# The key side's band moves from TensorE to GpSimd, and the values come one period later

## The reference, cut to what matters

```
h = shift_token(x); q, k, v = split(h @ wqkv)          # 8 heads of 64
q, k = rotary_xpos(l2norm(q) * qs, l2norm(k) * ksc)
sim  = einsum(q * 8, [keys of the window before, own window])   # windows of 64
sim  = where((i < j) | (i > j + 64) | (j == -1), -max, sim)     # the band
x    = x + (softmax(sim) @ v) @ wo
h    = layernorm(shift_token(x)) @ w1 + b1; a, g = split(h)
x    = x + (a * gelu(g)) @ w2 + b2
```

## Time and profile before

| | |
|---|---|
| median of the runs | 1264.93 us (1263.29 to 1266.61) |
| span of the profiled execution | 1264.4 us, 0.5 us under that median; its own device time is not listed apart |
| TensorE busy | 1158.7 us, 92% of the span |
| VectorE busy | 986.2 us, 78% |
| ScalarE busy | 829.0 us, 66% |
| GpSimd busy | 443.5 us, 35% |
| chain that ended last | TensorE 51% of the span, VectorE 4%, ScalarE 2%, issue 1% |

### The profile page before, as it was taken

How to read it: one execution, slowest core, us unless ns; L and a number is a source line. 1 busy time by engine, 2 the same in 40 slices (tenths; PEclk the granted TensorE clock), 3 DMA queues, 4 the chain that set the end, 5 groups by cost and what they waited for, 6 DMA issues and landing times.

```text
span 1264.4 us, 36707 instructions
## 1 busy us (share of the span) xinstructions
PE 1158.7 (92%) x15602; PEld 682.3 (54%) x15602; DVE 986.2 (78%) x1556; ACT 829.0 (66%) x1229; POOL 443.5 (35%) x582
## 2 busy tenths in 40 slices
PE   4498999899999999688999999999999999999985
PEld 3133434343435555455666666666666666666662
DVE  7868695868768888796877887788778877887755
ACT  3498898889887877535556656665666566656641
POOL 2203221211206447855533333333333333333310
PEclk8599999999999999988999999999999999999997
DMA  3113121020113331100201110111111111101102
GB/s 105 34 24 136 39 101 35 18 101 18 63 56 125 127 136 69 50 18 19 80 21 27 24 30 20 28 27 23 27 27 23 28 23 27 28 23 28 27 6 67
DMA packets 37329, 59.78 MB, mean 47 GB/s; under 512 B 6416, under 2 KB 12464, under 8 KB 37168
## 3 DMA queue, kind: packets, MB, share of 16 engines
q1 hardware_dynamic: 35760, 56.61, 15.1%
q10 hardware_dynamic: 1408, 0.84, 0.3%
HBM read 22.58 MB, written 16.78 MB: 31 GB/s over the span
## 4 chain that ended last, share of the span: by engine, by line
PE 51%; DVE 4%; ACT 2%; issue 1%; DVEq 0%; ACTq 0%
PE psum L1338 9%; PE psum L1474 7%; PE psum L1427 6%; PE psum L1449 5%; PE psum L1413 5%; PE psum L1348 4%; PE psum L1358 3%; PE psum L1500 3%; PE psum L1435 2%; PE psum L1398 2%; PE psum L1370 2%; ACT ffn_probs L1657 2%; PE psum L1404 1%; PE psum L1378 1%; PE psum L1466 1%
## 5 line engine op out<-in xcount | busy, mean ns | idle before, releaser
L829 ACT ACTIVATE att_probs<-psum 128x1024 f32<-128x1024 f32 (+2 forms) x384 | 350.6, 1005 | 50.7 <-PE psum L679 49.9
L1768 POOL TENSOR_TENSOR ffn_rot<-ffn_rot,ffn_rot_sin 128x512 f32<-128x512 f32 x128 | 160.1, 1272 | 373.3 <-DVE ffn_rot L1799 373.3
L723 PE MATMUL psum<-att_probs,att_v 128*32 128x256 f32 (+3 forms) x3712 | 227.1, 345 | 8.8 <-DVE att_probs L1021 6.2
L679 PE MATMUL psum<-att_q_stack,att_k_parts 64*128 64x512 bf16 (+4 forms) x1280 | 147.4, 295 | 25.1 <-ACT att_probs L829 18.3
L723 PEld LDWEIGHTS psum<-att_probs,att_v 128*32 128x32 f32 x3712 | 83.5, 109 | 81.1 <-issue 59.6
L1021 DVE TENSOR_TENSOR att_probs<-att_probs,att_causal_mask 128x1024 f32<-128x1024 f32 (+1 forms) x80 | 96.3, 1219 | 34.6 <-ACT att_probs L829 34.4
L679 PEld LDWEIGHTS psum<-att_q_stack,att_k_parts 64*128 64x128 bf16 x1280 | 44.8, 94 | 145.3 <-ACT att_probs L829 88.9
L1650 ACT ACTIVATE ffn_max_t<-psum 68x128 bf16<-68x128 bf16 x64 | 17.4, 273 | 156.9 <-PE psum L1386 156.7
L1657 ACT ACTIVATE ffn_probs<-psum 128x1024 f32<-128x1024 f32 x64 | 65.6, 1025 | 59.2 <-PE psum L1413 59.2
L1619 ACT ACTIVATE ffn_sq<-psum 128x512 f32<-128x512 f32 x128 | 74.6, 595 | 22.1 <-PE psum L1338 21.1
L610 POOL TENSOR_TENSOR att_rot<-att_qk 128x1280 f32<-128x1280 f32 x6 | 16.5, 2755 | 205.9 <-ACT att_qk L860 205.9
(11 more groups left out here) (222 smaller groups left out, 2442.4 us busy)
## 6 DMA issues: line engine op xcount, KB each, us to landing
ffn_v_back<-ffn_v SPq DMA_DIRECT2D x120, 130.0 KB, 2.4
att_q_stack<-q_rows SPq DMA_DIRECT2D x28, 512.0 KB, 3.6
q_rows<-att_q_high SPq DMA_DIRECT2D x21, 256.0 KB, 4.5
q_rows<-att_q_mid SPq DMA_DIRECT2D x21, 256.0 KB, 4.2
q_rows<-att_q_low SPq DMA_DIRECT2D x14, 256.0 KB, 4.1
xres<-in_hidden SPq DMA_DIRECT2D x4, 512.0 KB, 6.1
out<-ffn_qk_t SPq DMA_DIRECT2D x3, 512.0 KB, 3.2
tail_f_wqkv<-in_f_wqkv SPq DMA_DIRECT2D x1, 768.0 KB, 5.7
```

The lines of the kernel that those rows point to most:

```text
L679: ins = T.matmul(psum[:, banks[i] + at:banks[i] + at + width], k_parts[rows, p % 3, j, kt * P:(kt + 1) * P], q_stack[rows, turn % 2, j, q0 ...
L723: ins = T.matmul(psum[32 * g:32 * g + V_PAD, (4 + cc) * BANK + lo - cc * BANK: (4 + cc) * BANK + hi - cc * BANK], v[:, p % 4, kt, g, shift ...
L829: act.activation(probs[:, n % E_BUFS, 2 * j:2 * j + 2, 0:width], ps2((step % 2) * 2).rearrange("p (h c) -> p h c", h=2)[:, :, 0:width], AC ...
L1768: steps.did(pool.tensor_tensor(out, out, halves(k.rot_sin[:, n % 2, :])[:, :, 1 - half, :], ALU.add), g["added"] if half else None)
```

## The change

The four band matmuls of `key_scores` are gone, and `band_t_bf` with them. `exponentials` now runs on unmasked scores, and a new step of GpSimd, `hide`, multiplies each of the two halves of `probs` (128x512, read as 32-bit integers) by a table `seen` of zeros and ones; `value_products` waits for `hidden` in place of `exped`. Values, output transposes and output projection of a tile come one period later, the ring of value tiles has five places for four, and there are 72 periods for 71. On TensorE `project_v` and `max_transpose` now stand ahead of `project_qk`, and `key_scores` directly behind `query_scores`. ScalarE and VectorE have new orders too, the chunk's steps begin a period later (n - 7 for n - 6), and the tables of the second layer are made in three periods.

```diff
-RING = 4
+RING = 5
-PERIODS = STREAM + 7
+PERIODS = STREAM + 8
 def key_scores(n):
-    for side, block_n in CORNERS:
-        rows, c0 = SIDE_ROWS[side], (KEY_BANK + side) * BANK
-        form = (2 if t == 0 else 1) if block_n else 0
-        T.matmul(psum[SIDE_ROWS[block_n], c0:c0 + BANK], keep.ident_bf[rows, rows],
-                 widen(k.band_t_bf[rows, form:form + 1, :], [FD, SIDE_HEADS, P]),
-                 start=True, stop=True)
...
 def value_products(n):
-    pe.wait_ge(g["exped"], n + 1)
+    pe.wait_ge(g["hidden"], n + 1)
@@ TensorE, the list of a period @@
+    c, step = divmod(n - 7, CHUNK_TILES)
+    if live(n):       project_v(n)
+    if live(n - 2):   max_transpose(n - 2)
     if live(n):       project_qk(n)
     if live(n - 1):   qk_transposes(n - 1)
     if step == 0:     up_gated(c - 1, 1, n)
+    if live(n - 3):   value_products(n - 3)
+    if live(n - 4):   project_out(n - 4)
+    if step == 1:     x_transposes(c)
+    if step == 2:     xn_transposes(c)
     if step == 3:     up_gelu(c, 1, n); up_gelu(c, 2, n)
+    if step == 0:     up_gated(c - 1, 2, n)
+    if live(n - 3):   out_transposes(n - 3)
+    if step == 2:     up_gelu(c, 0, n)
     if live(n - 1):   query_scores(n - 1)
+    if live(n - 2):   key_scores(n - 2)
     if step == 3:     up_gated(c, 0, n)
     if step == 0:     down(c - 1, j)
@@ ScalarE, the list of a period @@
+    copy_v(n); copy_max(n - 2); squares(n); copy_qkt(n - 1)
     if step == 2:     copy_hn(c)
     if step == 3:     gelu(c, j)
+    copy_ot(n - 3)
+    head_roots(n); exponentials(n - 2)
     if step == 1:     row_roots(c)
@@ VectorE, the list of a period @@
+    normalise_heads(n - 1)
     if step == 2:     normalise_rows(c)
     rope(n)
+    norm_out(n - 3)
     if step == 0:     gate(c - 1, 1)
+    square_sums(n)
     if step == 0:     gate(c - 1, 2)
     row_maxima(n - 1)
@@ GpSimd @@
+    def hide(n):
+        pool.wait_ge(g["exped"], n + 1)
+        form = 1 if n % TILES == 0 else 0
+        for side in range(SIDES):
+            rows = k.probs[:, n % 2, side].bitcast(I32)
+            steps.did(pool.tensor_tensor(rows, rows, widen(k.seen[:, form:form + 1, :],
+                      [P, SIDE_HEADS, P]), ALU.mult), g["hidden"] if side else None)
...
     scale_heads(pool, steps, n, DVE_NORM, 2 * FH, g["k_rotated"])
+    if live(n - 2):
+        hide(n - 2)
```

More of the change, by code:

```diff
@@ L1336, in project_qk @@
                     pe.wait_ge(g["tail_state"], TAIL_EVACS * b)
-                for i in range(2):
-                    T.matmul(bank(QK_BANK + i), keep.xs[:, b, t * P:(t + 1) * P],
-                             k.w_qkv[layer][:, i * INNER:(i + 1) * INNER],
-                             start=True, stop=True).then_inc(g["qk_in_psum"], 1)
-            def project_v(n):
-                layer, b, t = place(n)
                 if n >= 1:
@@ L1566, in _ @@
                     up_gated(c - 1, 1, n)
+                if live(n - 3):
+                    value_products(n - 3)
+                if live(n - 4):
+                    project_out(n - 4)
+                if step == 1 and live_chunk(c):
+                    x_transposes(c)
+                if step == 2 and live_chunk(c):
+                    xn_transposes(c)
                 if step == 3 and live_chunk(c):
@@ L1749, in _ @@
             pool.memset(keep.xs[:, 2, 0:1], 0.0).then_inc(g["tail_edge"], 1)
-            for n in range(STREAM):
+            def hide(n):
+                pool.wait_ge(g["exped"], n + 1)
+                if n == 0:
+                    pool.wait_ge(g["bands_ready"], 1)
+                form = 1 if n % TILES == 0 else 0
+                for side in range(SIDES):
+                    rows = k.probs[:, n % 2, side].bitcast(I32)
+                    steps.did(pool.tensor_tensor(rows, rows, widen(k.seen[:, form:form + 1, :], [P, SIDE_HEADS, P]), ALU.mult),
+                              g["hidden"] if side else None)
+            for n in range(STREAM + 2):
                 if n == 3:
```

123 lines of the change are left out of this document (65 added, 58 removed).

## The result

The changed kernel takes 1320.49 us (median of 4 runs, 1317.71 to 1323.37), the kernel before in the same rounds 1265.43. The ratio is 1.0424 (95% interval 1.041 to 1.0438): slower by 55 us. The forecast was 1283 with a range of 1250 to 1310, so the sign was right and the size wrong.

A forecast was written before the change was run, and what follows sets the result against it. TensorE was taken to bound the kernel, with VectorE just fitting. On a 1264.4 us span, +15 steady, +5 end and -2 start gave 1282.4, with 0.5 more on the median 1283 us; range 1250 to 1310.

The forecast's parts named there:

- `hide`: GpSimd's two masking operations a tile: 1.25 us each, 2.5 together; `hide` or rope 0.8 to 1.2 late on meeting VectorE.
- just fit: Old order: TensorE has no hole, and VectorE's 9.68 us between two maxima fills the whole period.
- The band: Key side's band on TensorE: all 0.34 us a tile goes, 0.12 of it due to the change of form.
- that rival: GpSimd's integer product is dearer than the addition, 1.9 us an operation: about 1325 us; chance 0.15.
- Step 2: Period with up product and query scores ahead of the maxima: 10.95 us with the collision, before 9.68; the dearest step.
- Step 0: Period where late roots push `hide` and the values start at 5.0: 12.8 us, before 12.69.
- Steps 3 and 1: Step 3 10.9 us, `copy_ot` some 0.25 ahead of key scores; step 1 9.1, `project_v` waits for the maxima.
- the floor of 40.83: TensorE's work alone over a chunk's four periods: 10.66, 12.35, 8.48 and 9.34 us.
- the forecast's 43.75: Chunk of four periods with the collisions between GpSimd and VectorE, in us; 42.7 without them, 42.37 before.
- The forecast's own 1.38 a chunk: Steady loss with collisions, 43.75 against 42.37 us; given as +1.4, taken as +1.1, +15 us over 14 chunks.
- The end: Last tile's values wait for exponential and `hide`, plus one more period: +5 us, bounds +2 to +9.
- The start: First eight periods, where the exponential's wait ahead of the values is gone: -2 us, bounds -5 to +3.

The follow-up runs named there:

- A: Kernel before with the key side's four band matmuls left out and nothing in their place; 1255.98 us, ratio 0.9919.
- L: J with value products back behind the transposes and the output projection of tile n-4 behind the transposed maximum; 1276.72 us, ratio 1.0079.
- C: Changed kernel without `hide`, so the key side is unmasked and values wait for the exponential; 1297.41 us, ratio 1.0244.
- G: Changed kernel with the output transposes of tile n-4 early, right behind `project_qk`; 1298.72 us, ratio 1.0251.
- M: L with step 2's first up projection moved behind both query and key scores; 1265.1 us, ratio 0.9991.
- B: The change's new orders and later period, but the band stays on TensorE and there is no `hide`; 1308.73 us, ratio 1.0325.
- F: Changed kernel with the output projection of tile n-4 moved between query and key scores; 1356.47 us, ratio 1.0706.
- J: G with `project_qk` first, value products directly behind the transposed maximum, and `square_sums` ahead of `norm_out`; 1356.83 us, ratio 1.071.

## Why the prediction was wrong

The sign held, and the mechanism in outline: the reordering brought VectorE and ScalarE in front of TensorE in a part of every period, and TensorE's busy time fell. That both engines "just fit" in the old order isn't shown (A). What failed is where TensorE waits and what a wait costs: the wait for `copy_ot`, taken for one step, stands in three, and the slow restart behind every wait was put at nothing. By the prediction's own steps:

- *The band.* 0.34 a tile went, and the maxima's part is 0.22 directly behind the query scores in three of the four steps of L (0.38 in step 1, without a wait that the view lists). That 0.12 of it was due to the place is confirmed by A (0.35 behind a full matmul). By the rule of the Trainium skill that was cited for it ("TensorEngine Tiling (Array Packing)", section Key Properties), the trace agrees.
- *`hide`.* Forecast 1.25 us an operation, and slower where it meets VectorE. The 128 operations:

```profile
L1760 POOL TENSOR_TENSOR ffn_probs<-ffn_probs,ffn_seen x128: 1261/1272/1929, 559.0 to 1273.3; 128x512 int32<-128x512 int32 x128
```

  The integer product costs what the addition does, so that rival is out; that its 1325 lies near the measured time is chance (and its own terms, 14 times 3.5, give 1332). The collisions are there: two operations took 3.16 at 1012.40, while VectorE's scaling took 1.42 for 0.88. But TensorE waits less for them than forecast, 0.59 us a chunk (0.50 in step 2, 0.09 in step 0) and not some 1.5. The prediction's estimate by the Trainium skill ("GPSIMD Engine Reference", section 3.1) was 1.11 an operation; the measured 1.27 decides against it.
- *Step 2.* Forecast 10.95, measured 10.96, with its chain as told: values, output projection, copy, up product, query scores, maxima, `project_v`. That it fits to 0.01 is luck: the values start 0.4 us sooner than forecast (4.33 after `project_v` and not 4.75), and what comes behind the waits takes that back (1.15 for 1.08, 1.12 for 0.86, and 0.14 before `project_v` starts).
- *Step 0.* Forecast 12.8, measured 12.96, but for another reason. The forecast had 0.45 of waiting for `hide`; TensorE waits 0.09 for it and 0.21 for `copy_ot`, with 0.20 of restart. Without `hide` the step still takes 12.80 (C).
- *Steps 3 and 1: the failed step.* Forecast 10.9 and 9.1, measured 11.53 and 9.59. The prediction put it thus: "what is left is `copy_ot` behind three `gelu`, some 0.25 ahead of the key scores", and gave this wait to step 3 alone. It stands in steps 3, 0 and 1, with 0.34, 0.21 and 0.21 of idle and 0.20 of restart behind each: 1.36 a chunk for the forecast's 0.25. In step 1 I had output transposes, then query scores of 0.57, then key scores, and did not ask for the copy (0.61 and 0.14 to the start), although the wait for it is in the code. The wait of `project_v` for the maxima, which it had in steps 1 and 2, comes in step 2 alone, once a chunk. 0.63 + 0.49 + 0.16 + 0.01 is 1.29 a chunk above the forecast's 43.75, 18 us over 14 chunks. The forecast's own 1.38 a chunk is 19 more, which it rounded down to 15; together that makes the 37.9 above. G, by moving these calls, takes 1.38 off the three steps, 16 us in the stretch from tile 8 to 63 and 22 in all.
- *The restart.* I priced each wait by its idle time. Behind a wait, pieces cost 1.15 for 1.08 (values), 1.10 for 0.86 (`project_v`), 1.12 for 0.86 (up product), 0.42 for 0.22 (maxima's part). The view of the waits has 90 of them in 13 chunks, some seven a chunk, and with those under 0.15 us nine. The trace of before already had such a piece, the values behind the exponential of step 1:

```profile
1036.75 1.15 PE psum L1427 x32
```

  The changed kernel's chunk is 4.2 us above the floor of 40.83. Idle time of TensorE is 2.4 of it (my sum of the idle ahead of its pieces, mean of 12 chunks), less than the 2.9 that the forecast had added up. The other 1.8 are pieces longer than at the floor: the restarts above, and perhaps more, since M stands above the floor with hardly a wait. No run takes the restart away by itself, so its share of the 1.8 isn't shown.
- *The end.* Forecast +5, bounds +2 to +9; measured +18, 4 of it the moved step 0. The bounds counted `hide` once and the period's pieces as moved. It is paid twice, since the key scores of tile 63 stand behind the values of tile 62 in the queue, and the clock falls behind each. Thirty us behind tile 63's squares, columns as above:

```profile
1255.00:1265.00 10.00, 6.28 (x133) 5.67 (x131) 4.28 (x14) 2.17 (x5) 2.48 (x2) 0.84 0.01 2
1265.00:1275.00 10.00, 5.88 (x96) 4.62 (x94) 0.90 (x2) 4.26 (x5) 2.48 (x2) 0.84 0.00 0
1275.00:1285.00 10.00, 10.00 (x71) 6.76 (x69) 2.94 (x5) 3.14 (x4) 0.00 (x0) 0.72 0.01 2
```

  TensorE waits 7.2 us for `hide` there (3.5 and 3.7). In the 2.7 us behind the first wait the granted clock is 0.55, in the 4.0 us behind the second 0.50, and there the values take 2.00 and the output projection 2.01 for 1.09. C takes 8.8 us away; some 5 are left for the period itself, which I had at nothing.
- *The start.* Forecast -2, measured +4.5, of which 2.1 lie ahead of the change. From the feed-forward's first table load to tile 8 it is 91.9 us before, 94.2 in the changed kernel and 91.9 without `hide` (C). If the 2.0 that the period from tile 8 to 9 loses are counted in, C has the -2 of the forecast and `hide` takes 2.3 of it back, by one trace of each. By which wait was not followed.

That the rest of the steady loss comes from the order, and not from GpSimd, is shown by B and C (2.6 and 2.0 of the 2.7 us a chunk stay) and by L and M (it goes, with `hide` in place). That it is the loop through `norm_out` and the maxima is read from the chains and from G and F.

## What to carry to other kernels

When a reordering puts a consumer close behind a producer on an in-order engine, list every wait of the consumer, including those that only free a bank, and price the round trip in each period and not only where it is longest, with the restart behind it. Draw the loops that go through several engines: a piece of TensorE's work is free ahead of the operation that closes the loop and lengthens it behind, as the 1.09 us moved in F did (2.0 us a chunk dearer, although it was meant to cover a wait). An added period is not free at the end, some 5 us here, and an operation that one tile waits for can be paid there once for each tile that is left, with a slower clock behind. Compare stretches of two pipelines only when the same work lies in them.

## What was not expected of the hardware

- After a wait of 2.60 us inside the full stream the granted clock was 0.59 and a piece took 1.9 times its length (J, 2.00 for 1.08), while waits of 0.2 to 0.5 left the granted clock at 1.00 (changed kernel, 900 to 1060).
- GpSimd's 32-bit integer product is as fast as its fp32 addition: 1272 ns in the median for 128x512, against 1.25 us.
- A form change on TensorE costs 0.13 us and stays behind when the piece that first paid it is taken out (A).
